# Attention values for all heads computed token-major ahead of the head pairs, and fp32 attention products on the two column halves of TensorE

## The reference

```python
v = x @ wv.T + bv
q2 = (q @ wiq.T + biq).reshape(N, H, D).transpose(1, 0, 2)      # H = 16 heads of D = 64
k2 = (k @ wik.T + bik).reshape(N, H, D).transpose(1, 0, 2)
v2 = (v @ wiv.T + biv).reshape(N, H, D).transpose(1, 0, 2)
scores = jnp.einsum('hnd,hmd->hnm', q2, k2) * scale + mask[None]
attn = jax.nn.softmax(scores, axis=-1)
out = jnp.einsum('hnm,hmd->hnd', attn, v2)
out = out.transpose(1, 0, 2).reshape(N, OUT_F)
return out @ wo.T + bo
```

## Time and profile before

| | |
|---|---|
| median of 3 runs | 586.93 us (584.77 to 587.86) |
| the profiled execution | 584.88 us, its span 583.2 us |
| PE busy | 554.5 us (95%) |
| PE weight loads busy | 473.9 us (81%) |
| DVE busy | 381.9 us (65%) |
| ACT busy | 240.0 us (41%) |
| moved by DMA | 104.19 MB, 179 GB/s on average |

### The profile page before, as it was taken

One profiled execution on the slowest core, in us unless ns is written; L12 is line 12 of the kernel. 1 busy time (PEld: TensorE's weight loads), 2 busy tenths in 40 slices (PEclk: granted clock), 3 DMA queues, 4 the chain that ended last, 5 costly groups with the idle time before them and its releaser, 6 DMA issues.

```text
span 583.2 us, 8532 instructions
## 1 busy us (share of the span) xinstructions
PE 554.5 (95%) x3054; PEld 473.9 (81%) x3054; DVE 381.9 (65%) x747; ACT 240.0 (41%) x390; POOL 148.4 (25%) x161
## 2 busy tenths in 40 slices
PE   3989999999999999999999999999998998999985
PEld 3989997897999999999979999999997886633321
DVE  6688887865777346773548888888889886200114
ACT  3646554320243333353427556756576513320000
POOL 5627666851176500081000001001002010000020
PEclk9999999999999999999999999999998997999999
DMA  8655557530263554438523125416349688199943
GB/s 304 215 141 184 176 167 248 143 112 1 63 180 128 170 196 137 142 119 287 162 82 132 58 90 123 128 58 160 132 156 326 225 311 338 62 383 412 411 174 112
DMA packets 33778, 104.19 MB, mean 179 GB/s; under 512 B 5424, under 2 KB 9712, under 8 KB 33744
## 3 DMA queue, kind: packets, MB, share of 16 engines
q1 hardware_dynamic: 28224, 89.95, 44.6%
q0 software_dynamic: 5376, 13.29, 8.6%
q10 hardware_dynamic: 144, 0.52, 0.3%
HBM read 96.58 MB, written 5.60 MB: 175 GB/s over the span
## 4 chain that ended last, share of the span: by engine, by line
PE 80%; DVE 11%; ACT 4%; issue 3%; DMA 1%; POOL 0%; DVEq 0%; SPq 0%; ACTq 0%
PE ps L1604 41%; PE ps L1955 10%; PE ps L1797 6%; PE ps L1618 5%; DVE wsp L954 4%; PE ps L1901 2%; PE ps L1741 2%; PE ps L1751 2%; PE ps L1726 2%; PE ps L1688 2%; PE ps L1669 2%; PE ps L1761 2%; ACT wsp L660 1%; DMA tok<-in_x 1%; DVE big L954 1%
## 5 line engine op out<-in xcount | busy, mean ns | idle before, releaser
L1604 PE MATMUL ps<-big,wsp 128*128 128x384 f32 x1656 | 295.7, 336 | 3.2 <-DVE wsp L954 2.7
L1604 PEld LDWEIGHTS ps<-big,wsp 128*128 128x128 f32 x1656 | 286.0, 188 | 7.8 <-issue 5.3
L954 DVE TENSOR_TENSOR wsp<-raw,wsp 128x1024 fp32r<-128x1024 f32 x85 | 110.5, 1304 | 30.4 <-ACT wsp L660 29.5
L660 ACT ACTIVATE wsp<-raw 128x1024 fp32r<-128x1024 f32 x83 | 86.9, 1052 | 32.9 <-PE ps L1618 12.9
L569 POOL DMA_INDIRECT edge_table<-ef,eidx x48 | 56.0, 1167 | 33.0 <-DMA edge_table<-ef,eidx 19.2
L667 ACT ACTIVATE big<-ps,bias 128x384 f32 x24 | 14.0, 583 | 80.8 <-PE ps L1604 80.8
L1955 PE MATMUL ps<-blocks 128*64 128x512 f32 x192 | 43.8, 599 | 0.0
L965 DVE SCALAR_TENSOR_TENSOR big<-ps,bias,big 128x384 f32 (+1 forms) x24 | 14.8, 617 | 34.2 <-ACT big L667 33.5
L784 ACT ACTIVATE work<-work,snm 128x384 f32<-128x384 f32 x48 | 28.9, 604 | 16.1 <-DVE snm L1221 16.1
L1618 PE MATMUL ps<-wsp,big 128*128 128x512 f32 x144 | 33.2, 390 | 0.3 <-DVE wsp L954 0.3
L1618 PEld LDWEIGHTS ps<-wsp,big 128*128 128x128 f32 x144 | 26.9, 188 | 6.3 <-DVE wsp L954 0.8
(11 more groups left out here) (249 smaller groups left out, 715.3 us busy)
## 6 DMA issues: line engine op xcount, KB each, us to landing
raw<-in_w_stream SPq DMA_DIRECT2D x85, 512.0 KB, 4.1
blocks<-in_w_experts SPq DMA_DIRECT2D x64, 512.0 KB, 9.1
rowbuf<-in_rowb POOLq DMA_DIRECT2D x6, 512.0 KB, 6.6
raw_x<-in_w_stream SPq DMA_DIRECT2D x4, 512.0 KB, 6.3
slot_y<-rowbuf POOLq DMA_DIRECT2D x7, 256.0 KB, 5.7
tok<-in_x SPq DMA_DIRECT2D x3, 512.0 KB, 4.0
edges_a<-in_src_rows SPq DMA_DIRECT2D x8, 192.0 KB
edges_a<-in_dst_rows SPq DMA_DIRECT2D x8, 192.0 KB
```

Source lines behind the costliest of these rows:

```text
L660: nc.scalar.activation(wsp[:, 0, slot, :], raw[:, slot, :], ACT.Copy).then_inc(w_hi, 1)
L954: return nc.vector.tensor_tensor(dst, value, hi.bitcast(F32), ALU.subtract)
L1604: ins = nc.tensor.matmul(ps[:, bank, 0:N], wsp[:, a, slot, k * P:(k + 1) * P], moving[:, b, k, :], start=(k == 0 and n == 0), stop=(k == K ...
```

## The change

The second projection of v is done for all 16 heads at once, before the gate and up quarters. The activation v is stationary and the weights move, so that the values come out token-major. There are two groups of four quarters. Group 0 is split as whole quarters; group 1 is split in eight column chunks into the places in `wsp` that group 0's products have left. ACT copies the six results (128x512) out as plain fp32 into `v_rows`, three units of the buffer for expert blocks. The bias of v is added to the attention's output instead, where `out_part` splits it. The transposed probabilities are copied once, in plain fp32, into `probs_t`. `attend` multiplies both heads at once, in plain fp32, each with 64 stationary columns, into the lower and the upper 64 partitions of one bank. The pair loop has two quarters a round. The splits of two quarters go to `pt` and `x2_lo_c` instead of `wsp`, the rows of the stream are loaded in another order, the last wait of the hidden layer and the first wait of the output projection are cut into steps, and some expert blocks change their homes.

SP's queue:

```diff
-            for q in range(Q_PAIR0, Q_PAIR):
-                load(q * P, slot_of(q), q - RING + 1)
-            with sp.Fori(0, PAIRS - 1) as i:
...
+            for q in range(Q_PAIR0, Q_WO):
+                load(ROW_OF[q - Q_PAIR0] * P, slot_of(q), q - RING + 1)
...
-            sp.wait_ge(w_started, Q_WO - 1)
+            sp.wait_ge(w_started, Q_WO)
```

ACT's queue ahead of the pairs, from the last quarter of the projection of v:

```diff
+            prep(slot_of(Q_V), free=Q_V - 2)
...
+            for j in range(1, RING - 1):
+                prep(slot_of(Q_V + j), free=Q_V - 1)
             acc_part(qp[:, 0, :], everyone, bias[:, B_IQ:B_IQ + 1])
-            prep(slot_of(q_no.n))
+            prep(slot_of(Q_V + RING - 1), free=Q_V - 1)
             acc_part(kp[:, 0, :], everyone, bias[:, B_IK:B_IK + 1])
...
+            for k in range(KT):
+                act.wait_ge(v_chunk, k + 1)
+                ins = nc.scalar.activation(v_chunk_of(0, k), raw[:, :, k * P:(k + 1) * P], ACT.Copy)
...
+            prep(slot_of(Q_GU), RING)
+            prep(slot_of(Q_GU + 1), free=Q_GU + 1)
+            for group in range(2):
+                values(group)
+            prep(slot_of(Q_GU + 2))
```

DVE's queue in one round of pairs:

```diff
                 normalise(0)
-                acc_part(qp[:, 1, :], qp[:, 0, :], everyone, bias[:, bass.ds(p + B_IQ, 1)])
-                prep(3)
-                pt_part(0)
+                acc_part(qp[:, 1, :], qp[:, 0, :], everyone, bias[:, B_IQ + p:B_IQ + p + 1])
                 normalise(1)
-                acc_part(kp[:, 1, :], kp[:, 0, :], everyone, bias[:, bass.ds(p + B_IK, 1)])
-                prep(0 if last else 1)
-                head_sum(0)
-                pt_part(1)
+                prep(slot_of(q_no.n))
                 if not last:
                     if p % 2:
                         residual_statistics((p - 1) // 2)
                     else:
                         scaled((p - 2) // 2)
-                values(p)
-                prep(1 if last else 2)
-                head_sum(1)
-                values_lo()
+                prep(slot_of(q_no.n))
+                acc_part(kp[:, 1, :], kp[:, 0, :], everyone, bias[:, B_IK + p:B_IK + p + 1])
+                out_part(p - 1)
                 s_no.add()
-                maxima(0)
+                maxima(0, s_read if last else None)
                 maxima(1)
-                out_part(p - 1)
```

ACT's round is now: the exponentials of both heads, `acc_part` of q, one `prep`, both copies of transposed probabilities, one `prep`, `acc_part` of k, `out_part(p - 1)`. PE's queue:

```diff
+            def value_products(group, opened):
...
+                for k in range(KT):
+                    opened(k)
+                    for t in range(NT):
+                        for n, (a, b) in enumerate(PASSES):
+                            ins = nc.tensor.matmul(
+                                ps[:, v_bank(group) + t, :].rearrange("p (c n) -> p c n", n=P),
+                                feat[3][:, b, k, t * P:(t + 1) * P], v_chunk_of(a, k),
...
+            def first_split(k):
+
+                if k == 0:
+                    pe.wait_ge(w_lo, q_no.value + RING)
...
+            def attend(p):
+
+                pe.wait_ge(pt_out, pt_no.add(2))
                 bank = open_acc()
                 for mt in range(NT):
...
+                    for s in range(2):
+                        ins = nc.tensor.matmul(ps[s * DH:(s + 1) * DH, bank, 0:N], v_rows[mt][:, v_cols(p, s)],
+                                               probs_t[:, s, mt, :], start=(mt == 0), stop=(mt == NT - 1))
...
+            def pair(p):
+
+                first = Q_PAIR + 2 * (p - 1)
+                feature_major(slot_of(first), feat[1])
+                feature_major(slot_of(first + 1), feat[2], {2: lambda: transpose_probs(0), 4: lambda: transpose_probs(1)})
+                attend(p - 1)
+                pe.wait_ge(acc_free, acc.value - 1)
                 for t in range(NT):
...
+                    ins = score(t)
...
-            pe.wait_ge(s_max, HEADS - 1)
-            pe.wait_ge(out_lo, PAIRS - 2)
-            project_all(0)
+            project_all(0, scores_read)
             pe.wait_ge(s_max, HEADS)
```

More of the change, by code:

```diff
@@ L115, in slot_of, with stream_rows @@
 def slot_of(q):
-    if q < Q_PAIR:
-        return q % RING
-    if q < Q_WO:
-        return 1 + (q - Q_PAIR) % 3
-    return (q - Q_WO) % XRING
+    return q % RING if q < Q_WO + RING else q - Q_WO
+def stream_rows():
+    first = Q_PAIR0 + 2
+    pair = first + 2 * FHT + 1 + 3
+    values = [first + 2 * FHT] + [pair + 3 * p + 2 for p in range(PAIRS - 1)]
+    return ([Q_PAIR0, Q_PAIR0 + 1] + values + list(range(first, first + 2 * FHT)) +
+            list(range(pair - 3, pair)) + [pair + 3 * p + n for p in range(PAIRS - 1) for n in range(2)])
+ROW_OF = stream_rows()
 def up_blocks(p):
@@ L234, in graph_layer @@
         rowi = sb("rowi", [P, OVER + 1], I32)
-        vt = row_buf[:, 0:N]
+        v_rows = [blocks[:, U_V + t, :] for t in range(NT)]
         qp_row, kp_row = qp[:].rearrange("p a b -> p (a b)"), kp[:].rearrange("p a b -> p (a b)")
@@ L812, in mix_product @@
                     .then_inc(mix_normed, 1)
-            def pair(p, last):
+            def pair(p):
                 exps(0)
@@ L954, in lo, with prep @@
                 return nc.vector.tensor_tensor(dst, value, hi.bitcast(F32), ALU.subtract)
-            def prep(slot):
+            def prep(slot, into=None):
                 dve.wait_ge(w_hi, q_no.add())
-                lo(wsp[:, 1, slot, :], raw[:, slot, :], wsp[:, 0, slot, :]).then_inc(w_lo, 1)
+                high, low = (w_split(slot if into is None else into, part) for part in range(2))
+                lo(low, raw[:, slot, :], high).then_inc(w_lo, 1)
             def acc_part(dst, hi, rows, b):
@@ L1219, in maxima @@
                         scalar=3.0 * NONE, op0=ALU.add, op1=ALU.max, accum_out=smx[:, s, t:t + 1])
+                    if read is not None and t < NT - 1:
+                        ins.then_inc(read, 1)
                 then(ins)
@@ L1713, in _, with down_product @@
+            value_products(1, second_split).then_inc(v_ready, 1)
+            feature_major(RING, feat[0])
+            for q in range(Q_GU + 1, Q_DOWN):
                 feature_major(slot_of(q), feat[0])
-            feature_major(slot_of(Q_DOWN - 1), feat[3])
-            values_acc = acc.value
+            pe.wait_ge(v_out, 2 * NT)
+            def down_product(t, h, k):
+                blk = h * FHT + k
+                slot, kk = slot_of(Q_DOWN + blk // 2), blk % 2
+                for n, (a, b) in enumerate(PASSES):
+                    ins = nc.tensor.matmul(ps[:, 2 + 2 * t + h, :], pt[:, b, k, t * P:(t + 1) * P],
+                                           wsp[:, a, slot, kk * HALF:(kk + 1) * HALF],
+                                           start=(k == 0 and n == 0), stop=(k == FHT - 1 and n == 2))
+                    if t == 0 and n == 0 and blk in (0, 3, 4):
+                        ins.then_inc(w_started, 1)
+                return ins
@@ L1753, in attend @@
                 ins.then_inc(acc_ready, 1)
-            def scores():
-                for t in range(NT):
-                    for n, (a, b) in enumerate(PASSES):
-                        for s in range(2):
-                            rows = slice(s * DH, (s + 1) * DH)
-                            ins = nc.tensor.matmul(ps[:, 2 + 3 * s + t, 0:N], qp[rows, a, t * P:(t + 1) * P],
-                                                   kp[rows, b, :], start=(n == 0), stop=(n == 2))
-                ins.then_inc(s_ready, 1)
@@ L1783, in _, with score @@
-            pe.wait_ge(acc_free, values_acc)
-            transpose_values()
-            pe.wait_ge(down_sum, NT)
-            scores()
-            with repeat(pe, PAIRS - 2, {q_no: 3, acc: 6, norm_no: 2, pt_no: 2}):
-                pair()
-            pair()
+            def score(t):
+                for n, (a, b) in enumerate(PASSES):
+                    for s in range(2):
+                        rows = slice(s * DH, (s + 1) * DH)
+                        ins = nc.tensor.matmul(ps[:, 2 + 3 * s + t, 0:N], qp[rows, a, t * P:(t + 1) * P],
+                                               kp[rows, b, :], start=(n == 0), stop=(n == 2))
+                return ins
@@ L1792, in project @@
+            score(0)
+            pe.wait_ge(down_sum, NT)
+            for t in range(1, NT):
+                ins = score(t)
+            ins.then_inc(s_ready, 1)
+            for p in range(1, PAIRS):
+                pair(p)
             def project(h, t, j):
```

296 lines of the change are left out of this document (141 added, 155 removed).

## The result

The changed kernel takes 588.78 us (median of 17 runs, 587.51 to 589.93), the kernel before 585.54 us (median of its 17): a ratio of 1.0055, interval 1.0044 to 1.0066. That is +3.2 us, where the sum of the prediction had +3.2. The ratio lies just above the 0.5% that the prediction took as the least that a measurement tells from no change. The level forecast, 590.1, was 1.3 us higher because it stood on a median of three runs of the kernel before (586.93), where seventeen give 585.54. The profiled execution took 588.62 us, its span is 586.8.

A forecast was written before the change was run, and what follows sets the result against it. PE's own work plus its few waits was taken to bound the kernel. Terms 35.9 - 30.5 - 2.3 + 0.1 gave +3.2 us: 588.1 profiled, 590.1 as median; range 580 to 598, likeliest case 586 to 594.

The forecast's parts named there:

- the sum of the prediction: Whole kernel: 35.9 ahead of the rounds, -30.5 in them, -2.3 at the output projection, +0.1 last attend: +3.2 us.
- The level forecast: Whole kernel: a median of 590.1 us, with 588.1 for the profiled execution; chance 0.48.
- The values ahead of the pairs: Before the pair stage: 144 added products cost +33.2 us; one quarter product and three transpositions removed give -4.6.
- The opening: Before group 0's first value product: PE waits 4.5 us for DVE's fourth split, delayed by POOL's additions.
- The low clock behind it: Behind the opening wait: PE's clock falls to 1.2 GHz, costing +1.7 us (0 to 3).
- The hidden layer: Down product: PE waits 1.5 us for the last down quarter's split, no longer hidden by v's quarter product.
- A round: Pair loop: 15.1 us a round, including a new 0.7 us wait for head 1; seven rounds save 30.5 us.
- Rival 2: Pair rounds: no wait for head 1, 7 x 0.7 = 4.9 us less, 585.2; chance 0.12.
- Rival 3: Pair rounds: 0.7 us idling lowers the clock each round, 11.5 us more, 601.6; chance 0.12 shared with the non-overlapping halves.
- Rival 4: Attention products: array halves don't overlap, 8 x 1.95 = 15.6 us more, 605.7; chance 0.12 shared with the per-round low clock.
- The output projection: After the last scores: starting after one score tile leaves head 0's softmax as bound, 5.2 plus 0.1 against 7.6: -2.3 us.

The follow-up runs named there:

- the first group: The changed kernel as first measured against the kernel before: 588.78 us, ratio 1.0055.
- the control run: The changed kernel itself, unedited, measured again beside later variants: 590.40 us, ratio 1.0072 to the kernel before.
- three edits: Changed kernel with POOL's bias-row additions held back, head 1 normalised before q's sum, and last-down-quarter products put last: 576.75 us, ratio 0.9816 to the kernel before.

## Why the prediction was right

**The values ahead of the pairs, +33.2 and -4.6: right.** The 144 products take 32.8 us where the clock stayed up (263.37 to 296.13, additions held back), 0.4 less than by the row of the same shape. In the changed kernel it is 34.14 (266.11 to 300.25), and the difference of 1.4 is the low clock.

**The opening, +4.5: right** in cause and size (4.35). The held-back additions show the cause: 3.9 us of the wait went with the collision, 0.46 stayed. The Trainium skill (SBUF — State Buffer, Terms) describes this lock of the shared port for a whole instruction; the trace agrees, 3.42 and 3.01 us beside POOL, 1.22 without. That the loser waits in units of POOL's instructions let the wait be worked out ahead.

**The low clock behind it, +1.7: sized too low.** I charged a wait over twice as long the price of the 1.82 us wait. Six of seven profiles show 2.6 to 3.0, one 1.4, and the one that came with the result happened to be that one; the mean of the seven is 2.6. With it, taking the wait away is worth 3.9 + 2.6 = 6.5 us, against the 6.7 measured.

**The hidden layer, +1.5: right** as a wait (1.49), and worth 1.8 us of the stretch when taken away, since here too the overlap around the wait comes back. The measured gain, 0.47% or 2.8 us, has an interval of some 1.3 us to either side, and 1.8 lies in it.

**A round, 15.1: right** (15.07). The wait for head 1 was 0.45 instead of 0.7, but costs 0.66 of the round, and the attention product 2.09 instead of 2.15. Rival 2 was that this wait would not be there; making it go away gave 0.66 x 7 = 4.6 us of rows and 5.3 us of time, the 4.9 that the rival had. The copies of the values and the transfers showed no wait of PE, as argued: from 250 us to the output projection PE waits only at the places named here, and 0.5 us before the scores of pair 0.

**Rival 3, low clock in each round: wrong,** no stretch below full clock stands inside the rounds in any profile, though seven of them have 0.45 us of waiting in each round. **Rival 4, halves that don't overlap: wrong** as forecast, and the runs show how they do overlap. The price of that rival, 8 x 1.95, would have been too high even for products in head order: by the rows that costs 8 x 0.69 = 5.5.

**The output projection, -2.3: the number right, by luck in part, the reason half right.** The step said: head 0's softmax bounds, 5.2 us after the scores, against 7.6, the low clock in the old figure included. But in the kernel before the softmax itself was ready only 7.1 us after the scores (445.19 + 3.13 against 441.21), because of POOL's clearing. The wait that I credited is worth 0.9 us by itself, interval from 2.2 to nothing; the other half is a collision that the change took apart by moving a mix row. The row of 3.13 us stood in the trace before; only a reading of DVE beside POOL at that place would have shown it.

**The sum** came out as forecast because most terms were right, and in part by luck. The low clock behind the opening wait is by the mean of seven profiles 0.9 us dearer than charged, the 144 products are 0.4 cheaper, the two waits inside the stages cost a little more than they show. With the clock's mean the sum would be 4.1; the first group measured +3.2, the control run +4.2. Two groups of runs agree to about 1 us, so that the closeness of 3.2 to 3.2 means nothing beyond that.

**What decided the sign.** The change gives back 30.5 + 2.4 us and costs some 28 us of products, and ahead of the rounds 4.4 of waiting, 1.4 to 3.0 of clock and 1.8 at the down product; another 4.6 for a wait is inside the 30.5. Without the three waits, which the order of DVE's and PE's queues and POOL's place cause, it is 9.5 us faster than before by the medians of the group (586.21 and 576.75; 10.8 by the ratio) instead of some 3 to 4 slower. The kernel before, with the tile wait and the late clearing, stands at 0.9956, the changed one with three edits at 0.9816.

## What to carry to other kernels

When a step is moved forward, look for every pair of DVE and POOL instructions on fp32 tiles in SBUF that overlap at its new place: a split of 1.2 us took 3.4. Such a collision had been there all along (3.0 us in the kernel before) and became a wait only when PE had nothing else to do. Holding POOL back moves the collision to the next split, so see what waits for that one. Price the moved work by rows of the same shape, then the first wait of each stage by writing out the queue of the late engine. Add to a wait of several microseconds the low clock behind it (2.6 us on average behind 4.4 here), and to a short one the lost overlap (0.2 to 0.3 us here). Where an engine is freed by one edit and nothing moves, read the next limit at the same place; two limits that hide each other show only when both go.

## What was new about the hardware

- fp32 products with 64 stationary columns and 384 moving ones take 0.65 us each in their own half of the array (two loads, 0.33 us each), and the other half's run beside them at no cost: 8 records and 12 records both took 2.1 us. In head order it is 2.78, where two heads one after the other would be 6 x 0.65 = 3.9; the loads fit a second head that starts before the first has ended.
- The three divisions of 128x384 went from 1.08 to 3.13 us beside a POOL MEMSET of 1.73 us. It cost DVE 2.05 us, more than its own 1.73, which none of the runs explains. Held back, it took 1.4 us beside the next head's division, which took 1.62 us.
- The low clock behind one and the same wait of 1.2 us came in 4 of 14 executions, at 1.7 us each; behind the wait of 4.4 us it came in 7 of 7, at 1.4 to 3.0 us. Runs of one kernel spread over 2.4 to 6.3 us (five runs or more), and profiles of single executions can't be compared to better than about 3 us in the span. Stretches of them can.
